# Three rotating slots for block-diagonal queries and values, and a new order of the work on every engine

## The chip, the cores and the metric

The kernel runs on one core of a Trainium2 chip. The metric is device time in microseconds (us). Three runs of the kernel before took 477.31, 477.70 and 478.84 us, the median is 477.7 us.

## What is computed

x and ctx are (16, 256, 256) in float32, so there are T = 4096 tokens of D = 256 values, in 16 heads of 16. The two steps, cut to what matters:

```
q = layernorm(x); k = v = ctx                      # heads: (b, s, 16, 16)
scores = einsum('bsqd,bskd->bsqk', q, k) / 4       # per token, between its 16 heads
scores = where(tril(16, 16), scores, -1e18)
x = x + einsum('bsqk,bskd->bsqd', softmax(scores), v)
xf = layernorm(x)
top1 = argmax(xf @ gate_w.T + gate_b)              # one of 8 experts for each token
x = x + (relu(xf @ w1[e].T + b1[e]) @ w2[e].T + b2[e])  for e = top1
```

## The kernel before

**Attention.** The tokens are cut into 16 chunks of 256 (NC, CT), four chunks make a group. A token's scores are a 16 x 16 product of its own, so eight tokens are packed into one 128 x 128 matmul: the queries of eight tokens stand as 16 x 16 blocks on the diagonal of a tile whose other places are zero, and the values likewise. Every operand is split into a float16 value and its float16 remainder ("hi" and "lo"), and three products are added. TensorE makes a chunk's scores with 96 matmuls (L1111), VectorE and ScalarE do the softmax (L684 to L702, L539), GpSimd multiplies by the inverse (L1012), TensorE turns the weights (L1129), ScalarE and VectorE split them (L544, L706), and 96 more matmuls make the chunk's outputs (L1143). VectorE adds x (L716).

**The diagonal tiles.** ScalarE and GpSimd split queries and values into qv_hl (L475, L987 for queries, L493, L1003 for values). DMAs put them onto the diagonal. Each covers 16 partitions, so eight of them serve all 128: SyncE issues five, ScalarE three (LATER). There are three diagonal slots in the arena, which later holds an expert's weights. Slots 0 and 2 hold queries of odd and even chunks, slot 1 in the middle holds the values of every chunk but the last but one. A buffer's place beside its neighbour's lets one DMA of 64 KB (spread_part, L305) carry the values of chunk i and the queries of chunk i + 2. The first two chunks' queries (L311) and the last two chunks' values (L307) go alone, 32 KB each. The joint transfer waits until outputs of chunk i - 1 and scores of chunk i are done and both operands are split:

```
sp.wait_ge(s_v_hi, i + 1)
sp.wait_ge(s_v_lo, i + 1)
if i + 2 < NC:
    sp.wait_ge(s_pv, i)
    sp.wait_ge(s_q_hi, i + 3)
    sp.wait_ge(s_q_lo, i + 3)
    sp.wait_ge(s_qk, i + 1)
```

There is one buffer of halves for values: the cast of values i waits until values i - 1 have landed in the slot (L492). There are two for queries.

**Routing.** For each group TensorE turns the outputs (L1156) and makes the gate's logits (L1171, four quarters a group). VectorE does the second layer norm and picks the expert (choose()), TensorE counts (L1178 to L1186), GpSimd scatters rows of 128 tokens to a table sorted by expert (L1050). In three stages VectorE plans which expert each of the 39 tiles (NTILES) has (plans()).

**Experts.** A tile is 128 rows of one expert. SyncE fetches rows and biases (L451 to L457), ScalarE normalizes (L566), TensorE turns the rows (L1196), ScalarE and VectorE split them (L571, L906). Eight up units of six matmuls each (L1229) make 1024 hidden values in two halves (c = 0, 1). Each half passes VectorE with the bias (hiddens(), L915), ScalarE's relu (L580) and VectorE's remainder (rests(), L926). Eight down units of two matmuls (L1245, L1246) give the result, which VectorE scales and adds in two halves (results(), L940), and GpSimd stores (L1076).

**The order.** Each engine runs its instructions in program order. Its work is written as lanes: generators that yield a number before each step, and weave() always takes the lane whose number is least. For attention the numbers are tables in the code, by lane and chunk. For the experts they are a formula, tile_at(j) = 240.0 + 5.7 j with an offset for each step: rows are turned at + 0.6, up unit n stands at + 2.6 + 0.7125 n, down unit n at + 8.65 + 0.7125 n. So ups of tile j and downs of tile j - 1 alternate one by one, and the rows of tile j are turned among the last units of tile j - 1, two up units and three down units ahead of their first use. Numbers only order the steps; what a step waits for is in its semaphores. Nothing else in a lane depends on them.

The functions that the diff touches:

## Time and profile before

| | |
|---|---|
| median of 3 runs | 477.7 us |
| span of the profiled execution, first to last instruction | 492.6 us |
| time of the profiled execution around its span | not given |
| mean granted TensorE clock | 0.962 |
| TensorE busy | 402.1 us (82%) |
| VectorE busy | 346.3 us (70%) |
| GpSimd busy | 208.7 us (42%) |
| ScalarE busy | 177.5 us (36%) |
| moved by DMA | 69.39 MB in 105162 packets |

The engines are PE (TensorE matmuls), PEld (its weight loads, which overlap the matmuls), DVE (VectorE), ACT (ScalarE), POOL (GpSimd) and SP (SyncE). "SPq" and "ACTq" mark what an engine's queue does beside operations, such as issuing a DMA. An arrow "<-" in a name has the tile written on its left and what is read on its right; in brackets behind an instruction stand the time for which its engine sat idle before it and what ended that. L305 is line 305 of the kernel. The profiled span is longer than the median run.

### The profile page before, as it was taken

What the parts mean: (1) busy time and instruction counts of PE and PEld (TensorE: products, weight loads), DVE (VectorE), ACT (ScalarE), POOL (GpSimd) and SP (SyncE); (2) the same over time, 40 slices, a digit from 0 to 9 for tenths busy, and PEclk for the clock granted to TensorE, in tenths of its full rate; (3) what the DMA queues carried; (4) which work ended last, traced back from release to release, by engine and by line L of the source; (5) the groups of instructions that cost most, each with busy time, mean ns of one, the idle gap of its engine ahead of it and who ended that gap; (6) DMA issues with size and microseconds to landing.
All of it is one profiled execution on the core that took longest, in us unless ns stands there. A gap on an engine that the chain in (4) does not pass through costs nothing.

```text
span 492.6 us, 16316 instructions
## 1 busy us (share of the span) xinstructions
PE 402.1 (82%) x5967; PEld 338.3 (69%) x5967; DVE 346.3 (70%) x777; ACT 177.5 (36%) x317; POOL 208.7 (42%) x213
## 2 busy tenths in 40 slices
PE   0135868888888866897999999779999999999992
PEld 0025757887787765896887877557778877877871
DVE  7978969789945863477757877457666666766662
ACT  3343255542624221342434433224333333433420
POOL 8345374334673467523723242642333323233221
PEclk9999999999999999975699999889999999999998
DMA  8999578899685664377612232544333322222210
GB/s 282 414 305 218 135 170 241 212 259 260 160 220 119 152 167 107 106 173 181 207 45 67 68 76 81 185 131 155 90 68 77 77 62 62 69 60 61 84 31 0
DMA packets 105162, 69.39 MB, mean 141 GB/s; under 512 B 78077, under 2 KB 88190, under 8 KB 104576
## 3 DMA queue, kind: packets, MB, share of 16 engines
q1 hardware_dynamic: 75696, 56.67, 41.9%
q10 hardware_dynamic: 25984, 3.21, 4.6%
q0 software_dynamic: 3408, 8.46, 4.6%
q8 instruction: 53, 0.87, 0.7%
q14 instruction: 21, 0.17, 0.1%
HBM read 48.28 MB, written 12.57 MB: 124 GB/s over the span
## 4 chain that ended last, share of the span: by engine, by line
PE 55%; DMA 11%; SPq 9%; DVE 9%; issue 6%; POOL 5%; ACT 2%; ACTq 1%; another core or an unknown queue 1%; POOLq 0%; DVEq 0%
PE s_ps L1229 20%; SPq L305 8%; PE at_ps L1245 6%; DMA arena<-qv_hl 6%; PE pv_ps L1245 6%; PE pv_ps L1143 6%; PE s_ps L1111 3%; PE lg_ps L1171 3%; PE pv_ps L1246 3%; PE at_ps L1246 3%; POOL qv_hl L987 2%; PE tr_ps L1156 2%; DMA arena<-x 2%; PE st_ps L1196 2%; POOL k_hl L995 1%
## 5 line engine op out<-in xcount | busy, mean ns | idle before, releaser
L1229 PEld LDWEIGHTS s_ps<-arena 128*128 x1872 | 132.7, 99 | 52.2 <-issue 14.6
L1229 PE MATMUL s_ps<-arena 128*128 128x128 f16 x1872 | 158.6, 222 | 8.4 <-DVE arena L906 5.1
L915 DVE SCALAR_TENSOR_TENSOR arena<-arena,s_ps 128x512 f32<-128x512 f32 x78 | 53.6, 687 | 48.6 <-PE s_ps L1229 35.9
L1076 POOL DMA_INDIRECT result<-arena x39 | 38.8, 995 | 95.5 <-DVE arena L940 91.6
L1111 PEld LDWEIGHTS s_ps<-k_hl,arena 128*128 128x128 f16 x1536 | 54.3, 118 | 29.9 <-DMA arena<-qv_hl 22.1
L1111 PE MATMUL s_ps<-k_hl,arena 128*128 128x16 f16 x1536 | 54.7, 179 | 23.3 <-DMA arena<-qv_hl 19.3
L1143 PE MATMUL pv_ps<-a_hl,arena 128*128 128x16 f16 x1536 | 54.7, 179 | 19.7 <-DMA arena<-qv_hl 15.9
L1143 PEld LDWEIGHTS pv_ps<-a_hl,arena 128*128 128x128 f16 x1536 | 53.5, 118 | 22.8 <-DMA arena<-qv_hl 18.3
L1245 PE MATMUL at_ps<-arena,k_in 128*128 x160 | 60.9, 383 | 0.8 <-DVE k_hl L926 0.6
L1245 PE MATMUL pv_ps<-arena,x_in 128*128 x152 | 58.1, 383 | 0.1
L1069 POOL TENSOR_TENSOR arena<-arena 128x256 f32<-128x256 f32 x39 | 30.7, 786 | 60.7 <-DMA arena<-b 60.6
L580 ACT ACTIVATE k_in<-arena 128x512 f16<-128x512 f32 x40 | 25.2, 630 | 65.7 <-DVE arena L915 60.3
L580 ACT ACTIVATE x_in<-arena 128x512 f16<-128x512 f32 x38 | 23.9, 630 | 69.0 <-DVE arena L915 60.4
L898 DVE SCALAR_TENSOR_TENSOR arena<-arena 128x512 f16<-128x512 f32 x56 | 48.0, 926 | 0.8 <-ACT arena L558 0.7
L1246 PE MATMUL at_ps<-arena,k_hl 128*128 x160 | 43.8, 274 | 0.1
L1246 PE MATMUL pv_ps<-arena,x_in 128*128 x152 | 41.8, 275 | 0.0
L1050 POOL DMA_INDIRECT sorted_rows<-pay,slot_i x32 | 34.2, 1067 | 15.9 <-DVE slot_i L802 8.1
L558 ACT ACTIVATE arena<-arena 128x512 f16<-128x512 f32 x56 | 32.0, 621 | 17.4 <-DMA arena<-w 13.7
L926 DVE SCALAR_TENSOR_TENSOR k_hl<-arena,k_in 128x512 f16<-128x512 f32 x40 | 27.7, 693 | 11.0 <-ACT k_in L580 10.7
L1003 POOL TENSOR_TENSOR qv_hl<-v_in,qv_hl 128x512 f16<-128x512 f32 x16 | 21.6, 1353 | 30.6 <-ACT qv_hl L493 30.6
L926 DVE SCALAR_TENSOR_TENSOR x_in<-arena,x_in 128x512 f16<-128x512 f32 x38 | 26.9, 709 | 8.8 <-ACT x_in L580 8.5
L987 POOL TENSOR_TENSOR qv_hl<-x_in,qv_hl 128x512 f16<-128x512 f32 x16 | 22.1, 1384 | 20.7 <-ACT qv_hl L475 20.7
(143 smaller groups left out, 614.2 us busy)
## 6 DMA issues: line engine op xcount, KB each, us to landing
arena<-w SPq DMA_DIRECT2D x28, 512.0 KB, 6.1
arena<-sorted_rows SPq DMA_DIRECT2D x39, 130.0 KB, 2.4
arena<-b SPq DMA_DIRECT2D x39, 128.0 KB
arena<-qv_hl SPq DMA_DIRECT2D x70, 64.0 KB, 3.5
k_in<-k_t SPq DMA_DIRECT2D x16, 256.0 KB, 3.9
v_in<-v_t SPq DMA_DIRECT2D x16, 256.0 KB
arena<-x SPq DMA_DIRECT2D x4, 1024.0 KB, 12.1
o_sb<-x_r SPq DMA_DIRECT2D x16, 256.0 KB, 3.8
```

What stands on the lines that cost most here:

```text
L305: eng.dma_start(to, qv_hl[part, at].rearrange("p s b c u a -> p (s b) c u a")).then_inc(s_bd[i % 2], 16)
L580: eng.activation(h_hi[j % 2][:, c * HALF:(c + 1) * HALF], h_in[:, c], ACT.Relu).then_inc(s_h_hi, 1)
L898: eng.scalar_tensor_tensor(out=lo, in0=src, scalar=W_SCALE, in1=hi, op0=ALU.mult, op1=ALU.subtract).then_inc(s_w_lo, 1)
L915: eng.scalar_tensor_tensor(out=h_in[:, c].rearrange("p (k t) -> p k t", t=P), in0=bias, scalar=W_SCALE, in1=h_ps[c][:].rearrange("p (k t) ...
L926: eng.scalar_tensor_tensor(out=h_lo[j % 2][:, cols], in0=h_in[:, c], scalar=0.0, in1=h_hi[j % 2][:, cols], op0=ALU.max, op1=ALU.subtract). ...
L1050: eng.indirect_dma_start(out=sorted_rows, out_offset=bass.IndirectOffsetOnAxis(ap=slot_i[:, b:b + 1], axis=0), in_=pay[:, b, :], in_offset ...
L1076: eng.indirect_dma_start(out=out, out_offset=bass.IndirectOffsetOnAxis(ap=rows[:, r, :].bitcast(I32)[:, D + 2:D + 3], axis=0), in_=rows[:, ...
L1111: m = eng.matmul(s[:, n], q_bd[i % 2][:, n // 2, :, n % 2, q], k_hl[:, n, k, :], start=False, stop=(n, q) == (BLK - 1, 1))
L1143: m = eng.matmul(o[:, n], v_bd[i][:, n // 2, :, n % 2, v], a_hl[:, n, a, :], start=(n, a, v) == (0, 0, 0), stop=(n, v) == (BLK - 1, 1))
L1229: k = eng.matmul(o, weights_of(j, w + k_ * H + n * P, P), xt[:, j % 2, k_ * P:(k_ + 1) * P], start=k_ == 0 and w is HI_1 and xt is xt_hi, ...
L1245: eng.matmul(y[:], h_hi[j % 2][:, n * P:(n + 1) * P], weights_of(j, at, 2 * D), start=n == 0, stop=False)
L1246: k = eng.matmul(y[:, 0:D], h_lo[j % 2][:, n * P:(n + 1) * P], weights_of(j, at, D), start=False, stop=n == KH - 1)
```

## The change

Slots: diagonal[n] are the three slots of the arena, chunk i uses diagonal[i % 3], first for its queries and, once its scores are done, for its values. Queries and values of a chunk travel in eight DMAs of 32 KB each, with separate lanes (spread_queries, spread_values). Three semaphores count landings. SyncE issues five of each eight and ScalarE three, as before.

```
-        q_bd = diagonals[:, 2 * SLOT_BLOCKS:], diagonals[:, 0:SLOT_BLOCKS]
-        v_bd = [q_bd[0] if i == NC - 2 else diagonals[:, SLOT_BLOCKS:2 * SLOT_BLOCKS] for i in range(NC)]
+        SIDES = 3
+        diagonal = [diagonals[:, n * SLOT_BLOCKS:(n + 1) * SLOT_BLOCKS] for n in (1, 2, 0)]
...
         def queries_landed(i):
-            return s_bd[i % 2], 128 * (i // 2 + 1)
+            return s_bd[i % SIDES], 128 * (2 * (i // SIDES) + 1)
 
         def values_landed(i):
-            return s_bd[i % 2], 128 * (i // 2 + 2)
+            return s_bd[i % SIDES], 128 * (2 * (i // SIDES) + 2)
...
+        def spread_part(eng, i, n, halves_of):
             part, cols = slice(HD * n, HD * (n + 1)), slice(HEADS * n, HEADS * (n + 1))
+            eng.dma_start(diagonal[i % SIDES][part, :, cols], halves_of[part]).then_inc(s_bd[i % SIDES], 16)
...
+            def spread_queries():
+                for i in range(NC):
+                    yield
+                    if i < SIDES:
+                        sp.wait_ge(*((s_zero_0, 1), (s_zero, 1), (s_zero, 2))[i])
+                    else:
+                        sp.wait_ge(s_pv, i - SIDES + 1)
                     sp.wait_ge(s_q_hi, i + 1)
                     sp.wait_ge(s_q_lo, i + 1)
+                    for n in range(8 - LATER):
+                        spread_part(eng, i, n, q_hl[i % 2])
+
+            def spread_values():
+                for i in range(NC):
+                    yield
                     sp.wait_ge(s_v_hi, i + 1)
                     sp.wait_ge(s_v_lo, i + 1)
+                    sp.wait_ge(s_qk, i + 1)
                     for n in range(8 - LATER):
-                        spread_part(eng, i, n)
+                        spread_part(eng, i, n, v_hl)
```

ScalarE's lanes change in the same way. VectorE zeroes slot 1 instead of the other slot first. Three waits differ elsewhere: the last expert's weights (load_late and weights) wait for s_pv, NC - 1 instead of s_qk, NC; fetch() waits for s_pv, NC - 2 instead of NC - 1; and hiddens() has one wait more.

```
                         dve.wait_ge(s_up, 2 * j + c + 1)
                         dve.wait_ge(s_b1[j % 2], 16 * (j // 2 + 1))
+                        dve.wait_ge(s_h_lo, 2 * (j - 1) + c + 1)
```

Order: a table TIMES holds a number for each step of each lane of each engine, for the experts too, and weave() sorts by it. The numbers serve as order alone.

```
-def weave(*lanes):
-
-    due = [(next(lane, None), n) for n, lane in enumerate(lanes)]
...
+def weave(times, **lanes):
+
+    turns = sorted((t, n, k) for n, name in enumerate(lanes) for k, t in enumerate(times[name]))
+    lane = list(lanes.values())
+    for steps in lane:
+        next(steps)
+    for _, n, _ in turns:
+        next(lane[n], None)
+    assert all(next(steps, True) for steps in lane)
```

What the sorted table gives, where the text below speaks of it:

- TensorE, attention: outputs of chunk i - 2 or i - 1 still stand about the scores of chunk i, one or two chunks deep, as before. All four quarters of the last group's gate matmuls stand ahead of the first up unit (before: one ahead, three among the first tiles' units).
- TensorE, experts: up to tile 13 ups and downs mostly alternate. From tile 14 to tile 37 a tile is: turn the rows of tile j; downs 0 to 3 of tile j - 1; ups 0 to 3 of tile j; then down 4 of tile j - 1, up 4 of tile j, down 5, up 5, down 6, up 6, down 7, up 7; and the next tile's rows. In tiles 17, 25 and 33 the run of ups is shorter.
- VectorE, experts, about the turning of tile j's rows: first half of the result of tile j - 2, second hidden half of tile j - 1, remainder of the rows (L906). In every other tile the second half of that result stands between the hidden half and the remainder, in the rest behind it. Before, the remainder stood ahead of the hidden half.

## Rows read from the trace of the kernel before

**Rows 1.** The page, chain that ended last, shares of the span by line

```profile
PE s_ps L1229 20%; SPq L305 8%; PE at_ps L1245 6%; DMA arena<-qv_hl 6%; PE pv_ps L1245 6%; PE pv_ps L1143 6%; PE s_ps L1111 3%; PE lg_ps L1171 3%; PE pv_ps L1246 3%; PE at_ps L1246 3%; POOL qv_hl L987 2%; PE tr_ps L1156 2%; DMA arena<-x 2%;
```

**Rows 2.** Busy us of each engine by stage, then clock, DMA share, GB/s

```profile
33.00:241.00 208.00, 166.44 (x3340) 152.73 (x3340) 154.83 (x366) 80.67 (x139) 104.64 (x89) 0.94 0.73 183
241.00:338.00 97.00, 89.58 (x966) 71.99 (x966) 67.17 (x167) 33.14 (x63) 39.46 (x45) 0.95 0.35 102
338.00:482.00 144.00, 142.18 (x1653) 111.72 (x1650) 95.62 (x180) 52.89 (x99) 43.93 (x49) 1.00 0.27 71
```

**Rows 3.** TensorE's waits from 35 to 240 us: us, times, longest

```profile
PE pv_ps L1143 <- DMA arena<-qv_hl: 15.9, 7, 4.4
PE s_ps L1111 <- DMA arena<-qv_hl: 8.0, 3, 3.6
```

**Rows 4.** The chain from 103 to 133 us: start, us, what

```profile
110.94 3.39 PE pv_ps L1143 x96
...
114.46 0.60 SPq L305
...
118.19 3.47 DMA arena<-qv_hl
...
121.71 3.38 PE pv_ps L1143 x96
```

**Rows 5.** Issues of spreading DMAs: median landing; on SyncE ns least/median/most

```profile
arena<-qv_hl SPq DMA_DIRECT2D x70, 64.0 KB, 3.5
...
arena<-qv_hl SPq DMA_DIRECT2D x18, 32.0 KB, 4.0
...
L305 SPq DMA_DIRECT2D arena<-qv_hl x70: 597/748/3080, 37.1 to 213.3; - x70
...
L307 SPq DMA_DIRECT2D arena<-qv_hl x10: 597/609/851, 219.9 to 230.7; - x10
```

**Rows 6.** Groups of instructions: the two steps that split the values

```profile
L493 ACT CAST qv_hl<-v_in 128x512 f16<-128x512 f32 x16 | 12.7, 791 | 18.9 <-DMA arena<-qv_hl 9.7 <-DMA v_in<-v_t 9.2
...
L1003 POOL TENSOR_TENSOR qv_hl<-v_in,qv_hl 128x512 f16<-128x512 f32 x16 | 21.6, 1353 | 30.6 <-ACT qv_hl L493 30.6
```

**Rows 7.** Timeline of TensorE where two up units stand in a row

```profile
244.51 0.97 PE L1229 MATMUL s_ps<-arena 128*128 128x128 f16 x12
245.32 1.90 PE L1171 MATMUL lg_ps<-gate_bd,o_sb 128*128 128x64 f32 x8
```

**Rows 8.** Timeline about the turning of one tile's rows in the steady part

```profile
380.50 0.50 PE L1229 MATMUL s_ps<-arena 128*128 128x128 f16 x6
380.84 0.38 PE L1245 MATMUL at_ps<-arena,k_in 128*128 x1
...
381.50 0.39 PE L1196 MATMUL st_ps<-ident,arena 128*128 128x128 f32 x2
381.72 0.38 PE L1245 MATMUL at_ps<-arena,k_in 128*128 x1
...
381.92 0.37 ACT L571 CAST arena<-st_ps 128x256 f16<-128x256 f32 x1 [0.19 <-PE st_ps L1196]
...
382.37 0.42 DVE L906 TENSOR_TENSOR arena<-st_ps,arena 128x256 f16<-128x256 f32 x1
...
383.24 0.69 DVE L915 SCALAR_TENSOR_TENSOR arena<-arena,s_ps 128x512 f32<-128x512 f32 x1 [0.45 <-PE s_ps L1229]
...
383.85 0.88 DVE L940 SCALAR_TENSOR_TENSOR arena<-at_ps,arena 128x256 f32<-128x256 f32 x2
...
387.01 0.39 PE L1196 MATMUL st_ps<-ident,arena 128*128 128x128 f32 x2
```

**Rows 9.** Timeline where TensorE waits for the remainder of a tile's rows

```profile
323.20 0.37 ACT L571 CAST arena<-st_ps 128x256 f16<-128x256 f32 x1 [3.09 <-remote]
...
323.60 0.42 DVE L906 TENSOR_TENSOR arena<-st_ps,arena 128x256 f16<-128x256 f32 x1 [2.77 <-ACT arena L571]
...
324.39 0.55 PE L1229 MATMUL s_ps<-arena 128*128 128x128 f16 x6 [2.48 <-DVE arena L906]
```

481 lines of the change are left out of this document (259 added, 222 removed), and 105 rows, old and new, of tables (TIMES, act, op1).

## Prediction

> **What bounds the kernel now.** I read the chain of work that ended last first, because it names what the end of the program hangs on. Besides TensorE it is made of the transfers that spread queries and values into the block-diagonal tiles, and of SyncE issuing them [rows 1]. Then the busy times by stage [rows 2]. From the first scores (33 us) to the first expert tile (241 us) TensorE is busy for 166.4 of 208 us, so 41.6 us are idle; from 241 to 338 us 7.4 of 97 are idle; after that 1.8 of 144. So there are two stages with different limits: attention, where TensorE waits, and the expert tiles, where almost nothing but TensorE's own stream counts.
>
> The waits of TensorE inside attention come next: 15.9 us before outputs and 8.0 us before scores, both on the spreading transfers [rows 3], together 23.9 of the 41.6 us. The chain in a stretch of attention shows why [rows 4]: outputs of one chunk end, SyncE then issues five transfers (from 114.46 to 118.8 us), the last lands 3.47 us after its issue, the next outputs run for 3.38 us and end, and so on. From one outputs to the next it is 121.71 - 110.94 = 10.77 us. The code has the reason: the values of all chunks but one share one diagonal slot, so the transfer of a chunk's values waits for the outputs of the chunk before (the wait on s_pv in spread()), and the queries of the chunk after next ride in the same transfer and wait as well.
>
> **What the change does to attention.** Three slots rotate. A chunk's queries go into slot i mod 3, and its values into the same slot once its scores are done. Outputs of chunk i-1 no longer hold up the values of chunk i, so the loop of [rows 4] is cut. This is the gain. Its bounds: at most the 23.9 us of [rows 3], at least nothing, because other loops have nearly the same length. The values still have a single buffer of halves: ScalarE's cast of chunk i waits for chunk i-1's values to have landed. That loop is cast 0.79 us, GpSimd's remainder 1.35 us [rows 6], five issues at 0.61 us and a landing of 4.0 us [rows 5], 9.2 us against 10.8. With 16 chunks the difference of 1.6 us is 25 us, the same size as the upper bound; but TensorE's own work is 166.4 / 16 = 10.4 us a chunk [rows 2], so most of the rest would have to run without a gap.
>
> The price is in the issues. Before there are 14 chunks of 8 joint transfers, 16 of first queries and 16 of last values, 144; after there are 2 x 16 x 8 = 256. A transfer of 32 KB takes SyncE 0.61 us to issue by the median, one of 64 KB 0.75 us, and the smallest are the same 0.60 us [rows 5]: halving a transfer hardly shortens its issue. SyncE goes from 70 x 0.75 + 18 x 0.61 = 63 us to 160 x 0.61 = 98 us, 35 us more; ScalarE from 56 to 96 issues, 40 x 0.61 = 24 us more, on top of 80.7 us of operations in this stage [rows 2]. Neither queue is full in 208 us, but both are in order: on ScalarE three issues (1.8 us) stand ahead of exponentials and of the halves of the weights, on SyncE five (3.1 us) ahead of loads of keys, values and x. A wait for scores ahead of each group of value transfers holds up all that is queued behind it. Cover that lies beside TensorE's work now is used up; gone altogether, the 24 us of ScalarE would be the loss. I take a gain of 7 us for attention, about a third of [rows 3]: nearer to the lower end, because the other loops and the issues follow so closely.
>
> The page on DMA of the Trainium skill (DMA: Bandwidth & Descriptors, section Rules for kernel authors) speaks against the split: it advises to coalesce small transfers, since under 64 KB one pays mostly overhead. The trace agrees in so far as a landing of 32 KB takes 4.0 us against 3.5 us for 64 KB [rows 5]; by the rule alone attention would lose instead of gaining, which is the fourth case below.
>
> **What the new order does to the expert tiles.** This part has nothing to do with slots. Until now TensorE alternates one up unit (six matmuls) with one down unit of the tile before, and turns the next tile's rows in between, two up units and three down units ahead of their use. A unit of up takes 0.34 us in that alternation (380.50 to 380.84), a tile 387.01 - 381.50 = 5.51 us [rows 8]. In the new order, from tile 14 to tile 37, a tile is: turn its rows, four downs in a row, four ups in a row, then four ups alternating with four downs. Two costs come out of it.
>
> First, ups in a row. Only the start of the expert stage shows them at full clock: two units take 245.32 - 244.51 = 0.81 us, 0.405 each [rows 7], 0.07 more than in the alternation. Three of four pay it: 0.2 us a tile.
>
> Second, the rows are turned only four downs ahead of their use. From the start of the turning, ScalarE's copy starts after 0.42 us, VectorE's remainder after 0.87 us, and it ends at 1.29 us [rows 8]; TensorE resumes about 0.37 us after the end of that operation where it has been waiting for it (323.60 + 0.42 = 324.02 against 324.39) [rows 9], so at 1.66 us. The turning (381.50 to 381.72) and four downs (0.32 us each by the rest of a pair, 381.50 - 380.84 = 0.66 less 0.34) fill 0.22 + 4 x 0.32 = 1.50 us. On VectorE a hidden half of 0.69 us stands in front, started some 0.2 us after the turning at the earliest, and half of a result (0.44 us) ahead of it; in every other tile the second half of the result (0.44 us) comes between hidden and remainder too. VectorE then reaches the remainder at about 1.0 us or 1.44 us, it ends at 1.4 or 1.86, and TensorE resumes at 1.8 or 2.2 us. Against 1.50 that is 0.3 and 0.7 us of idle TensorE, 0.5 us on average. Both costs together are 0.7 us a tile; the lower bound is nothing, if starts overlap more than these rows show. I take 0.5 us a tile, nearer to the rows, times 24 tiles: 12 us more.
>
> The other parts. Three quarters of the last group's gate matmuls move ahead of the first tile. It is the same work, up to 1.90 us a quarter [rows 7], on an engine that is busy on both sides of the boundary: no cost, but the first tile starts some 5 us later for it. The added wait on s_h_lo in hiddens() is for something that VectorE itself finished two operations before: nothing; were it not done, a tile would pay a gap of some 0.1 us. The late loads wait for the last outputs but one instead of the last scores, which costs a few us of lead before the last expert's weights; the expert inputs no longer wait for those outputs, which gives as much. At two tiles TensorE waits some 2.5 us for a remainder of rows, behind 3.09 us of ScalarE for which the trace names no engine [rows 9]; I keep these in the sum unchanged and put their 5 us into the range.
>
> **The sum.** -7 + 12 + 0 = +5 us. The profiled execution's span is 492.6 us, so 497.6; nothing of what lies around the span is shown. The median of the runs is 477.7 us, 14.9 us less than the span; I put the same +5 on it: **483 us**.
>
> **The cases.**
> 1. The forecast: attention gains about 7 us, the late order costs about 12. 483 us, by itself 478 to 488. Chance 0.40.
> 2. It ends faster: the shared slot is the one thing that held attention, TensorE's idle time there falls by 15 us of the 23.9, and the late order costs only 0.17 us a tile (4 us): 477.7 - 15 + 4 = 467 us. For it: the unbroken repetition of issue, landing, outputs in [rows 4]. Against: the 9.2 us loop of the value halves, and the rows turned late. It decides if value transfers are issued within 2 us of the scores' end and the tile's pitch stays below 5.7 us. Chance 0.33.
> 3. The wait takes another form: issues on ScalarE and SyncE eat all that the slots give, attention stays as it is, and the tiles cost 0.6 us each: 477.7 + 14 = 492 us. For it: 24 us more issues on an engine that is in the softmax chain. Against: that engine is idle for over a third of the stage. Chance 0.14.
> 4. The halved transfers land later, each by the 0.5 us between the two sizes in [rows 5]. With two landings a chunk on the path, 16 us more in place of the 7 us gained, and half the tiles' cost: 477.7 + 16 + 6 = 500 us. That is what the rule of the skill would give. Chance 0.05.
> 5. Both terms are equal, or the change does not do what it says: with the same in-order queues the rotation gives no depth and the new tile order costs nothing. 478 us. Chance 0.08.
>
> Within 0.3% (about 1.4 us) is what a measurement of this kernel cannot tell from no change. Faster by more: case 2 and a little of the others, 0.34; within: 0.09; slower: 0.57. The range runs from case 2 to case 3, 466 to 494 us; what lies outside is case 4 and the far end of case 2, with the 5 us of [rows 9] in it.
>
> **What would show it right or wrong.** In the profile after: TensorE's waits on the spreading transfers between 35 and 240 us fall from 23.9 to below 12 us, and softmax or ScalarE's casts appear in their place; the first up unit starts near 239 us: 7 us gained against the 241 us of before, 5 us of gate matmuls put ahead of it. From tile 14 on the turnings stand 5.9 to 6.1 us apart instead of 5.51, with TensorE idle for VectorE's remainder of rows in each second tile. If the pitch stays at 5.5 us, the second term is wrong and the kernel is faster; if the first up unit starts at 244 us or later, the first term is wrong.

## The result, and the profile after

The changed kernel takes **511.9 us** (median of 4 runs, 508.7 to 514.4) where the kernel before took 478.3 us beside it (4 runs, 477.3 to 481.2): a ratio of 1.068, 95% interval 1.062 to 1.073. The forecast was 483 us with a range of 466 to 494. The sign was right and the size was not: 34 us instead of 5, and 18 us beyond the end of the range. The ratios here and below compare the means of the kernels' runs in the fast state alone, so they are not the quotients of the medians beside them.

One thing had to be cleared up first. The profile shown of before has a span of 492.6 us, some 16 us more than its ordinary runs leave room for (a profiled run of the changed kernel took 508.7 us for a span of 507.0, so 1.7 us lie around it). A third profile of the kernel before (`before_third`, below) has a span of 480.6 us with a run of 482.4 us; it is the one to compare with. In the text "before" is that profile where a row of it is shown.

The page of the changed kernel, the chain that ended last, by engine and by line:

```profile
PE 57%; SPq 13%; DMA 10%; issue 5%; DVE 5%; ACT 4%; POOL 3%; ACTq 2%; POOLq 0%; DVEq 0%
PE s_ps L1379 22%; SPq L511 7%; PE at_ps L1395 7%; PE pv_ps L1395 6%; PE pv_ps L1295 5%; PE lg_ps L1321 4%; DMA arena<-qv_hl 4%; PE at_ps L1396 3%; PE s_ps L1265 3%; PE pv_ps L1396 3%; DMA arena<-w 3%; ACTq L511 2%; PE st_ps L1346 2%; PE tr_ps L1307 1%; ACT arena L731 1%
```

Against [rows 1] the landing of the spreading transfers has gone from 6% to 4%, their issue on SyncE (now L511) is 7% where it was 8%, and ScalarE's issues of them have appeared with 2%. Busy times by stage of the changed kernel (attention up to the first up, then to the turning of tile 14, then to the last downs), columns as in [rows 2]:

```profile
33.00:249.00 216.00, 171.87 (x3371) 158.27 (x3372) 155.88 (x353) 86.90 (x149) 108.47 (x91) 0.68 0.72 178
249.00:334.50 85.50, 83.25 (x927) 64.87 (x927) 63.26 (x161) 28.90 (x55) 36.82 (x41) 0.99 0.38 116
334.50:497.00 162.50, 156.68 (x1664) 117.61 (x1662) 98.51 (x179) 50.98 (x100) 49.28 (x51) 1.00 0.22 59
```

The same three stages of before, third profile:

```profile
33.00:238.50 205.50, 164.90 (x3339) 151.92 (x3337) 155.86 (x366) 81.58 (x140) 104.00 (x89) 0.83 0.74 184
238.50:323.70 85.20, 84.13 (x938) 69.02 (x939) 65.73 (x164) 32.38 (x61) 38.39 (x44) 0.97 0.38 112
323.70:471.70 148.00, 144.49 (x1688) 114.36 (x1684) 97.07 (x184) 53.71 (x101) 45.11 (x51) 1.00 0.28 73
```

In attention TensorE is idle for 216.0 - 171.9 = 44.1 us, before for 205.5 - 164.9 = 40.6. The last stage is the surprise: it is 14.5 us longer for the same work, and TensorE counts as busy for 12.2 us of it. Matmuls that follow one another slowly count as busy (the 24 of the tile shown below do, 2.02 us for what takes 4 x 0.33 = 1.3 us where ups and downs alternate), so the pitch of the tiles shows the loss and the idle time doesn't.

The yardstick for all that follows is the start of the turning of a tile's rows on TensorE, for tiles 3, 14 and 38 (by tile 3 all gate matmuls are done in both kernels, so the order of these no longer matters; what other work stands on either side of tile 3 comes below):

| profile | first up | tile 3 | tile 14 | tile 38 | mean step 3 to 14 | mean / median step 14 to 38 |
|---|---|---|---|---|---|---|
| before, third profile | 238.5 | 260.7 | 323.7 | 461.1 | 5.73 | 5.73 / 5.55 |
| changed, first profile | 249.3 | 262.7 | 334.5 | 488.1 | 6.53 | 6.40 / 6.45 |
| changed, second profile | 250.7 | 265.0 | 336.6 | 491.2 | 6.51 | 6.44 / 6.45 |

The second profile of the changed kernel (span 510.0 us, run 511.7 us) lies at its median. From before to it: 4.3 us up to tile 3, 8.5 us from tile 3 to 14, 17.2 us from tile 14 to 38, together 30.0 us; behind tile 38 it is 0.6 us quicker, which leaves the 29.4 us between the two spans. The medians lie 29.9 us apart in the job of that profile and 33.6 us in the first; 3.7 us of the first job's difference are in no profile compared here.

The first part is the least certain. Tile 3 comes between 262.7 and 269.3 us in the eight profiles of kernels that have the changed kernel's order up to it, so the 4.3 could be 2 to 9 us. And it is made of two parts: the first scores start 2.3 us later (at 35.1 us against 32.7, behind the first queries' transfer), and from there to the last outputs it is 4.3 us more (207.1 against 202.9 us). Ahead of tile 3 the changed kernel then makes 2.3 us good, in part because it has less to do there: three turnings of the last group's outputs, 0.45 us each, stand behind tile 3 instead of ahead of it.

What TensorE waits for in the changed kernel from 35 to 240 us (us in total, times, longest), the rows that answer to [rows 3]:

```profile
PE pv_ps L1295 <- DVE a_hl L870: 12.4, 6, 3.3
PE at_ps L1282 <- POOL a_sb L1166: 12.2, 5, 4.4
PE s_ps L1265 <- POOL k_hl L1151: 4.8, 2, 3.0
PE s_ps L1265 <- DMA arena<-qv_hl: 3.7, 3, 1.6
...
PE pv_ps L1295 <- DMA arena<-qv_hl: 0.7, 1, 0.7
```

The same rows of before, third profile:

```profile
PE pv_ps L1143 <- DMA arena<-qv_hl: 17.5, 9, 4.1
PE s_ps L1111 <- DMA arena<-qv_hl: 8.9, 3, 5.2
PE at_ps L1129 <- POOL a_sb L1012: 4.5, 3, 2.3
...
PE pv_ps L1143 <- DVE a_hl L706: 1.8, 1, 1.8
...
PE s_ps L1111 <- POOL k_hl L995: 0.4, 1, 0.4
```

The waits for the transfers fell from 23.9 us (26.4 in the third profile) to 4.4, as the slots should make them; the softmax, its weights and the halves of the keys took the place, 12.4 + 12.2 + 4.8 = 29.4 us where they had been 1.8 + 4.5 + 0.4 = 6.7. Who waits for the spreading transfers now is told by their own line in the changed kernel:

```profile
L511 SPq DMA_DIRECT2D arena<-qv_hl x160: 585/612/2157, 26.8 to 227.5; - x160
L511 ACTq DMA_DIRECT2D arena<-qv_hl x96: 592/632/1851, 26.3 to 223.4; - x96
...
  ACT qv_hl L680: 33.3, 12
```

L680 is ScalarE's cast of the values. It waits 33.3 us, 12 times, for the one buffer of value halves; before, it waited for the joint transfers (L305) 10.2 us, 8 times. So the wait that was cut on TensorE came back on ScalarE, ahead of the exponentials and the casts of the weights in its queue.

One tile of the changed kernel from the turning of its rows on (start, us, engine, operation):

```profile
379.27 0.39 PE L1346 MATMUL st_ps<-ident,arena 128*128 128x128 f32 x2
...
379.48 0.68 DVE L1071 SCALAR_TENSOR_TENSOR arena<-arena,s_ps 128x512 f32<-128x512 f32 x1
379.70 0.37 ACT L744 CAST arena<-st_ps 128x256 f16<-128x256 f32 x1 [1.57 <-PE st_ps L1346]
...
380.08 0.42 DVE L1096 SCALAR_TENSOR_TENSOR arena<-pv_ps,arena 128x256 f32<-128x256 f32 x1
...
380.41 0.41 DVE L1061 TENSOR_TENSOR arena<-st_ps,arena 128x256 f16<-128x256 f32 x1
...
381.19 2.02 PE L1379 MATMUL s_ps<-arena 128*128 128x128 f16 x24 [0.22 <-issue]
383.10 0.38 PE L1395 MATMUL at_ps<-arena,k_in 128*128 x1
...
385.74 0.39 PE L1346 MATMUL st_ps<-ident,arena 128*128 128x128 f32 x2
```

VectorE's remainder (L1061) stands behind a hidden half (L1071) and half of a result (L1096), ends at 380.82, and TensorE's first up starts 0.37 us later, just as read from [rows 9]. What the forecast did not have is what follows: the four ups take 383.10 - 381.19 = 1.91 us, 0.48 each, not 0.405.

### The profile page after: what moved, and what is told of

It is laid out like the page before. It is cut to its first block, busy times and chain, and to the rows that moved or that the text cites. A ratio compares the mean times of both kernels' runs of the same rounds, so it can differ in the third digit from the quotient of the medians.

```text
span 507.0 us, 16482 instructions
## 1 busy us (share of the span) xinstructions
PE 415.4 (82%) x5967; PEld 342.4 (68%) x5967; DVE 343.9 (68%) x777; ACT 175.1 (35%) x317; POOL 214.4 (42%) x213
## 3 DMA queue, kind: packets, MB, share of 16 engines
q1 hardware_dynamic: 77360, 56.74, 40.6%
## 4 chain that ended last, share of the span: by engine, by line
PE 57%; SPq 13%; DMA 10%; issue 5%; DVE 5%; ACT 4%; POOL 3%; ACTq 2%; POOLq 0%; DVEq 0%
PE s_ps L1379 22%; SPq L511 7%; PE at_ps L1395 7%; PE pv_ps L1395 6%; PE pv_ps L1295 5%; PE lg_ps L1321 4%; DMA arena<-qv_hl 4%; PE at_ps L1396 3%; PE s_ps L1265 3%; PE pv_ps L1396 3%; DMA arena<-w 3%; ACTq L511 2%; PE st_ps L1346 2%; PE tr_ps L1307 1%; ACT arena L731 1%
## 5 line engine op out<-in xcount | busy, mean ns | idle before, releaser
L1379 PEld LDWEIGHTS s_ps<-arena 128*128 x1872 | 129.1, 97 | 46.1 <-issue 18.7
L1379 PE MATMUL s_ps<-arena 128*128 128x128 f16 x1872 | 153.6, 219 | 6.2 <-issue 6.1
L1071 DVE SCALAR_TENSOR_TENSOR arena<-arena,s_ps 128x512 f32<-128x512 f32 x78 | 53.3, 684 | 50.5 <-PE s_ps L1379 50.4
L1228 POOL DMA_INDIRECT result<-arena x39 | 43.8, 1124 | 96.5 <-DVE arena L1096 95.1
L1295 PE MATMUL pv_ps<-a_hl,arena 128*128 128x16 f16 x1536 | 53.7, 179 | 14.5 <-DVE a_hl L870 12.4
L1395 PE MATMUL at_ps<-arena,k_in 128*128 x160 | 57.4, 379 | 0.9 <-DVE k_hl L1082 0.8
L1395 PE MATMUL pv_ps<-arena,x_in 128*128 x152 | 55.0, 378 | 0.8 <-issue 0.2
L1396 PE MATMUL pv_ps<-arena,x_in 128*128 x152 | 41.4, 272 | 0.0
L1082 DVE SCALAR_TENSOR_TENSOR k_hl<-arena,k_in 128x512 f16<-128x512 f32 x40 | 29.3, 734 | 14.2 <-ACT k_in L753 13.9
L1082 DVE SCALAR_TENSOR_TENSOR x_in<-arena,x_in 128x512 f16<-128x512 f32 x38 | 28.5, 750 | 14.9 <-ACT x_in L753 13.2
L1144 POOL TENSOR_TENSOR qv_hl<-x_in,qv_hl 128x512 f16<-128x512 f32 x16 | 20.8, 1300 | 28.4 <-ACT qv_hl L664 28.4
L1158 POOL TENSOR_TENSOR qv_hl<-v_in,qv_hl 128x512 f16<-128x512 f32 x16 | 21.7, 1355 | 26.2 <-ACT qv_hl L680 26.0
```

The lines of the kernel that those rows point to most:

```text
L1071: eng.scalar_tensor_tensor(out=h_in[:, c].rearrange("p (k t) -> p k t", t=P), in0=bias, scalar=W_SCALE, in1=h_ps[c][:].rearrange("p (k t) ...
L1082: eng.scalar_tensor_tensor(out=h_lo[j % 2][:, cols], in0=h_in[:, c], scalar=0.0, in1=h_hi[j % 2][:, cols], op0=ALU.max, op1=ALU.subtract). ...
L1228: eng.indirect_dma_start(out=out, out_offset=bass.IndirectOffsetOnAxis(ap=rows[:, r, :].bitcast(I32)[:, D + 2:D + 3], axis=0), in_=rows[:, ...
L1295: m = eng.matmul(o[:, n], diagonal[i % SIDES][:, n // 2, :, n % 2, v], a_hl[:, n, a, :], start=(n, a, v) == (0, 0, 0), stop=(n, v) == (BLK ...
L1379: k = eng.matmul(o, weights_of(j, w + k_ * H + n * P, P), xt[:, j % 2, k_ * P:(k_ + 1) * P], start=k_ == 0 and w is HI_1 and xt is xt_hi, ...
L1395: eng.matmul(y[:], h_hi[j % 2][:, n * P:(n + 1) * P], weights_of(j, at, 2 * D), start=n == 0, stop=False)
```

## The experiments

Times of a kernel are compared with runs of the kernel before in the same job. That kernel took 480 to 483 us (medians) in all of these jobs but the first, where it was 499.3 us (492.6 to 509.2; each job ran on a chip of its own); so for that job the ratios count. It is the job of the first three rows, its seven runs of the kernel before scattered over 17 us, and these three ratios are the least certain. The ratio of fixed_ups reaches down to 1.020.

| kernel | median us | before beside it | ratio, 95% interval |
|---|---|---|---|
| slots_alone | 526.8 | 499.3 | 1.062 (1.051 to 1.073) |
| new_tail_on_before | 524.2 | 499.3 | 1.059 (1.046 to 1.071) |
| old_tail | 513.8 | 499.3 | 1.035 (1.025 to 1.045) |
| after_again | 511.2 | 481.3 | 1.062 (1.055 to 1.069) |
| rows_earlier | 499.9 | 481.3 | 1.042 (1.036 to 1.048) |
| units_in_turn | 528.1 | 481.3 | 1.100 (1.094 to 1.107) |
| both_turns | 514.0 | 481.3 | 1.068 (1.061 to 1.075) |
| old_tail_again | 498.0 | 482.6 | 1.035 (1.026 to 1.044) |
| fixed_ups | 496.2 | 482.6 | 1.029 (1.020 to 1.037) |
| issues_on_sync | 555.4 | 482.6 | 1.154 (1.145 to 1.162) |
| halves_alone | 506.2 | 480.2 | 1.056 (1.051 to 1.061) |
| rows_earlier_all | 501.5 | 480.2 | 1.041 (1.033 to 1.048) |
| old_tail_240 | 503.1 | 480.2 | 1.048 (1.044 to 1.053) |
| earlier_and_fixed | 496.8 | 480.2 | 1.035 (1.029 to 1.040) |
| before_four | 480.7 | 481.3 | 0.999 (0.995 to 1.003) |
| after_four | 511.2 | 481.3 | 1.061 (1.054 to 1.067) |

### The kernel before and after, profiled again

No edit. The kernel before, twice:

> The kernel before, profiled a second time. Its first profiled execution has a span of 492.6 us, while its runs take 478. If that execution was an odd one (theory: the stretches from 187 to 199 and from 309 to 330 us, in which tiles took 10 us instead of 5.5, are an accident of it), this span lies at 475 to 480 us, the tiles come every 5.5 to 5.8 us from the first on, and the difference to the changed kernel's span of 507.0 is some 30 us. If they belong to the kernel, the span is again 490 or more and the runs' difference of 33 us isn't seen in the traces.

> The kernel before, profiled a third time. Its two profiles so far have spans of 492.6 and 501.6 us, while seven runs in each of two jobs took 477 to 483 us. Theory 'stalls': its two tiles of 10 us near 310 to 330 us and the one of 8 to 13 us near 250 us are in every execution; then the span is again over 490 us. Theory 'chip': where runs take 478 to 483 us the profiled span is 476 to 482 us, and tiles 11 and 12 take 6 to 7 us there.

The first of them ran on the slower chip: a span of 501.6 us, first up at 246.8, and again two steps of 12.1 and 7.9 us at tiles 11 and 12. The second: 480.6 us, and there these two steps take 5.6 and 5.9 us. So the long steps in [rows 9] belong to some executions and not to the kernel. In both of these steps, and in those of [rows 9], an engine stands for 3 to 6 us and the trace names no other engine that it waits for. From the profile on the slower chip:

```profile
313.65 4.72 another core or an unknown queue
318.39 0.38 ACT arena L571
...
321.40 5.75 another core or an unknown queue
327.18 0.70 DVE arena L915
```

GpSimd is issuing scatters of rows, one behind another, in just these stretches (seven of them start between 313.8 and 327.2 us), but what connects the two stays open. The two steps make 9.2 us of the 12.0 by which the first profile's span exceeds the third's, and 8.5 of the 21.0 for the profile on the slower chip; the rest lies elsewhere.

> The changed kernel once more, beside runs of the kernel before that took 499 us in the last job and not 478. If the chips differ by a factor, the ratio is again 1.06 to 1.07 (530 us beside 499); if what is slow on the other chip is a stretch that only the kernel before has (two tiles of 10 us at 310 to 330 us, which the changed kernel's first profile doesn't show), it is 510 to 515 us and a ratio near 1.03.

The ratio came out as the first time, 1.062 against 1.068: the size of the loss is the kernel's.

### The parts one by one: slots, attention's order, tail's order

`slots_alone` is the kernel before with the slots and the split transfers, each lane keeping its old numbers:

```diff
+                    if i < SIDES: sp.wait_ge(*((s_zero_0, 1), (s_zero, 1), (s_zero, 2))[i])
+                    else: sp.wait_ge(s_pv, i - SIDES + 1)
...
-                eng.matmul(... q_bd[i % 2] ...)
+                eng.matmul(... diagonal[i % SIDES] ...)
```

> The kernel before with three diagonal slots and a chunk's queries and values in transfers of their own, every engine's lanes in the order of before. Theory 1 (the new order of the expert lanes costs the time, the slots don't): 470 to 482 us, with TensorE's waits on DMA in the attention below 12 us instead of 23.9. Theory 2 (the slots and the halved transfers cost it: twice as many issues on ScalarE and SyncE): 495 us or more, with the loss before 240 us.

`new_tail_on_before` gives the expert lanes of the kernel before the order of the changed one:

```diff
-                        yield tile_at(j) + 2.6 + UNIT * n
+                        yield turn("PE", "ups", KH * j + n)
```

> The kernel before with the lanes of the expert tiles on ScalarE, VectorE, GpSimd and TensorE in the order of the changed kernel; two slots, the transfers and the attention's order as before (and the one wait that VectorE needs with this order). Theory 1: 503 to 515 us, tiles 6.3 to 6.5 us apart. Theory 2: 475 to 485 us. If the two parts only cost together (the tail's order needs the attention's), it is 480 to 500 us.

`old_tail` is the changed kernel with the opposite edit, the formula of before in the tables, from t0 = 232:

```diff
+    TIMES["PE"]["expert_inputs"] = at(0.6)
+    TIMES["PE"]["ups"] = at(*(2.6 + unit * n for n in range(8)))
+    TIMES["PE"]["downs"] = at(*(8.65 + unit * n for n in range(8)))
```

> The changed kernel with the lanes of the expert tiles alone (fetches, turnings, ups, downs and what VectorE, ScalarE and GpSimd do for them) back in the regular order of before, 5.7 us a tile, an up and a down in turn; the slots, the transfers and the new order of the attention stay. Theory 1 (the expert lanes' order costs nearly all: 0.87 us x 38 tiles = 33 us): 474 to 484 us, tiles 5.5 us apart. Theory 2 (the attention's part of the change costs it): 500 us or more, tiles 5.5 us apart but the first ups later than 250 us.

> The changed kernel with the expert lanes back in the regular order, once more: the first time it ran beside a kernel before of 499 us (ratio 1.035), and its profile had a single wait of 14 us for the diagonal of queries near 205 us. If that wait is the order's own (the expert lanes out of the attention leave it so), the ratio is again 1.03 or more. If it was the chip's, the ratio is 1.00 to 1.02, which leaves the tail's order as the cause of 20 us and more.

The tail's order alone costs 1.059, nearly the whole loss of 1.062 to 1.068: its steps from tile 14 to 38 are 6.44 us, as in the changed kernel, and it is slow from tile 3 on, which is taken up below. Taking the order away gives the steps back (`old_tail_again`: 5.70 mean, 5.57 median). So from tile 14 on the cause is the order of the expert lanes. Each expectation that put the other part at nothing was wrong, though: with the old tail the loss is still 1.035 in two jobs, 7.0 us up to tile 3 and 8.9 us from tile 3 to 14. (The wait of 14 us that the second expectation speaks of is at the very start, ahead of the first scores at 35 us, where before waits for 11.0 us; I had read its place wrongly. Their difference is the late start of the first scores.)

The parts don't add either: the tail's order alone costs 1.059 and the slots alone 1.062, both with the new order of attention 1.062 to 1.068. The slots in before's order cost 1.062 by themselves. The chain of `slots_alone` between 33 and 240 us was 24% SyncE's issues of spreading transfers and 6% ScalarE's; before it is 15% and not among the first dozen entries.

### The price of the issues

`halves_alone` has no new slots. Each joint transfer of 64 KB goes as two of 32 KB, at the same place and under the same waits:

```diff
-                eng.dma_start(to, qv_hl[part, at].rearrange("p s b c u a -> p (s b) c u a")).then_inc(s_bd[i % 2], 16)
+                for s in (at.start, at.start + 1):
+                    to = diagonals[part, s * SLOT_BLOCKS:(s + 1) * SLOT_BLOCKS, cols]
+                    eng.dma_start(to, qv_hl[part, s]).then_inc(s_bd[i % 2], 16)
```

> The kernel before with each diagonal transfer of 64 KB issued as two of 32 KB, the next queries and the values, one behind the other where the one was; two slots, every wait and every lane as before (112 issues more: 70 on SyncE, 42 on ScalarE). Theory 'issues': three slots in before's order cost 6 per cent for these issues alone, 20 to 30 us here too (500 to 512 us). Theory 'slots' (waits and places of the new lanes in the old order cost it, an issue is hidden): 478 to 486 us. Theory 'landing' (two transfers of 32 KB land later than one of 64 KB): attention waits on DMA grow from 26 us on TensorE, without SyncE on the chain.

506.2 us: 26 us for 112 issues, as the theory of the issues had it. The landing doesn't explain it. Issue and landing lines of `halves_alone`:

```profile
L306 SPq DMA_DIRECT2D arena<-qv_hl x140: 596/614/1723, 37.7 to 232.3; - x140
L306 ACTq DMA_DIRECT2D arena<-qv_hl x84: 592/649/1429, 37.7 to 229.3; - x84
...
arena<-qv_hl SPq DMA_DIRECT2D x158, 32.0 KB, 2.3
```

and of before, third profile:

```profile
L305 SPq DMA_DIRECT2D arena<-qv_hl x70: 597/814/4408, 37.2 to 210.3; - x70
L305 ACTq DMA_DIRECT2D arena<-qv_hl x42: 592/654/2121, 37.2 to 207.2; - x42
```

A half lands 2.3 us after its issue, where the whole took 3.5 [rows 5] (the profile has a landing for half of the issues; in slots_alone, where the halves don't go in pairs, it is 2.8 us, and for the changed kernel the page has none). But a half takes 0.61 us to issue and the whole took 0.75 to 0.81. For SyncE's five parts of a chunk that is 10 x 0.61 - 5 x 0.75 = 2.4 us more of issuing, less the 1.2 us by which the last part lands sooner: 1.2 us a chunk by these medians, some 16 us in 14 chunks. It is an estimate, and it leaves a part of the loss to what it doesn't have, such as the 42 more issues on ScalarE. TensorE's waits on these transfers grow from 26.4 to 42.5 us:

```profile
PE pv_ps L1144 <- DMA arena<-qv_hl: 29.5, 8, 7.3
PE s_ps L1112 <- DMA arena<-qv_hl: 13.0, 3, 4.5
```

and SyncE's issues rise to 31% of the chain between 33 and 240 us. The tail is that of before (median step 5.56 us against 5.55), and tile 3 comes at 281.6 us against 260.7: 20.9 of the 22.6 us between the two spans (503.2 and 480.6) are lost ahead of it. `slots_alone` has as many issues as the changed kernel and three slots, and costs the same as `halves_alone` within the intervals, so in before's order the third slot gave nothing back that the runs show.

`issues_on_sync` moves ScalarE's three issues of eight to SyncE (`LATER = 3` becomes `LATER = 0` in the changed kernel):

> The changed kernel with all eight transfers of a diagonal issued by SyncE, none by ScalarE (five and three before). Theory 'issues eat the gain': SyncE's 80 to 96 more issues at 0.65 to 0.7 us each are on the path, and the attention ends 20 to 50 us later (530 us or more). If instead ScalarE's issues are what holds back its casts and exponentials, the attention ends earlier than at 241 us and the time falls below 508 us.

555.4 us, 44 us more, for 96 issues moved: SyncE's issues become 61% of the chain between 33 and 240 us, and the first up starts at 292.3 us. ScalarE, freed of its issues, gains nothing by it, since its casts wait for the transfers:

```profile
L511 SPq DMA_DIRECT2D arena<-qv_hl x256: 585/611/2080, 28.5 to 270.6; - x128
...
  ACT qv_hl L680: 76.8, 14
```

`before_four` and `after_four` move one issue of eight the other way (`LATER = 4`):

> The kernel before with the eight transfers of a joint diagonal issued four by SyncE and four by ScalarE, where it was five and three; no more transfers than before. SyncE is on the chain of the attention for 15 per cent of it, ScalarE's queue hardly. Theory 'issues on SyncE are the path': 16 issues fewer there, 14 of them in the loop of a chunk at 0.61 to 0.8 us each, give up to 9 us, 470 to 477 us: faster than both kernels. If ScalarE's added issues hold up its casts by as much, it is 478 to 486 us.

> The changed kernel with four of the eight issues of a diagonal on ScalarE instead of three. All eight on SyncE cost 44 us more than five. Theory 'SyncE's issues are the path' on this side too: 32 issues less on SyncE give 3 to 10 us, 501 to 508 us. If ScalarE is by now as full, 511 to 518 us.

Both are the same as their parents within the interval. Taking 16 issues off SyncE was expected to give up to 9 us and gave nothing, so the price of an issue is not one of SyncE's queue alone: what SyncE is spared, ScalarE's queue pays for. Three and five was not tried, and no version that I ran beats the kernel before.

### Inside a tile: late rows, ups in a row, or the sequencer

Three edits of the changed kernel, all from tile 14 on. `rows_earlier` turns the rows two up units sooner, as before did, and leaves the runs of four:

```diff
+    for j in range(14, 39):
+        turn[j] = up[8 * (j - 1) + 6] - 0.5
+        rest[j] = hidden[2 * (j - 1) + 1] - 0.5
```

> The changed kernel, from tile 14 on with the next tile's rows turned two up units earlier on TensorE (and their remainder taken ahead of the second hidden half on VectorE); the four ups in a row stay. Theory 'late rows': this is what makes the 6.40 us of a tile out of 5.52, and they fall to 5.7 or below, 15 us off the end. Theory 'ups in a row': the four ups take 0.48 us each in a row and 0.33 us of time in turn with a down, so the tile keeps its 6.1 to 6.4 us and the end moves by 6 us at most.

`units_in_turn` interleaves the four downs and the four ups behind the turning, and leaves the turning late:

```diff
+        turns = sorted(up[a:a + 4] + down[b:b + 4])
+        down[b:b + 4], up[a:a + 4] = turns[0::2], turns[1::2]
```

> The changed kernel, from tile 14 on with the four downs and the four ups behind each turning taken in turn (down, up, down, up) and not four and four; the rows are turned where the change has them. Theory 'ups in a row': 0.6 us a tile come back, 25 x 0.6 = 15 us. Theory 'late rows': the first up now stands behind one down instead of four, waits for the rows 1 us longer, and the tile takes 6.4 us or more, up to 7.2.

`both_turns` has both:

> Both of these edits together, which is the regular order of before on TensorE from tile 14 on. Either theory: tiles of 5.5 to 5.7 us from tile 14 on, 17 to 21 us off the end. If the tiles keep 6.2 us or more, it is neither, and the order of VectorE's or ScalarE's lanes holds them.

`fixed_ups` takes the register arithmetic out of the ups (every tile's first layer uses expert 0's place):

```diff
-                                k = eng.matmul(o, weights_of(j, w + k_ * H + n * P, P), xt[...
+                                at = w + k_ * H + n * P
+                                k = eng.matmul(o, arena[:, at:at + P], xt[...
```

> The changed kernel, in which every tile's first layer takes its weights from the place of expert 0 at fixed addresses (so the result's first layer is that of another expert); everything else, the order too, stays. An up unit is then 12 instructions on TensorE's sequencer instead of 16. Theory 'ups in a row are bound by the sequencer': the four ups fall from 1.9 to 1.3 us, the tile from 6.40 to 5.8 us, 15 us off the end. Theory 'late rows' alone: the first up still waits for the rows, the four behind it run at 0.33 us each for want of register work, and what is gained is this alone, 0.3 to 0.6 us a tile. If ups are bound by the matmuls themselves, the time stays at 511 us.

> The changed kernel with the rows turned earlier from tile 14 on and the first layer's weights of expert 0 at fixed addresses (another expert's first layer is computed). Each edit alone took 0.53 us off a tile of 6.44 us. Theory 'one fault' (the rows arrive late, TensorE's sequencer stands at the first up and its register work for four ups in a row comes after it): together they give little more than each alone, 5.6 to 5.9 us a tile, 493 to 497 us. Theory 'two faults': they add up, 5.4 us a tile, 484 to 488 us.

| steps from tile 14 to 38, us | mean | median |
|---|---|---|
| before, third profile | 5.73 | 5.55 |
| changed (after_again) | 6.44 | 6.45 |
| rows_earlier | 5.92 | 5.75 |
| fixed_ups | 5.91 | 5.87 |
| earlier_and_fixed | 5.89 | 5.59 |
| both_turns | 6.43 | 6.33 |
| units_in_turn | 7.00 | 7.00 |

By the medians, which leave out single long steps: late rows are worth 6.45 - 5.75 = 0.70 us a tile, and the run of four 5.75 - 5.55 = 0.20 us. "Late rows" is the main cause, and "ups in a row" as a cause of its own is only the 0.20. That is 0.90 us a tile, though the 24 tiles lost 17.2 us, 0.72 a tile: before has single long steps there (its mean is 0.18 us above its median) and the changed kernel hardly has. By the means, late rows are 6.44 - 5.92 = 0.52 us and the run 5.92 - 5.73 = 0.19. How much ScalarE has to wait for the turned rows says it in one line each, before, changed (first profile) and rows_earlier:

```profile
  ACT arena L571: 9.1, 35
```

```profile
  ACT arena L744: 51.1, 37
```

```profile
  ACT arena L756: 27.6, 37
```

(engine and line that waited for the turning, us, times). In `rows_earlier` the four ups stand in a row as in the changed kernel, but take 350.23 - 348.65 = 1.58 us, 0.395 each, not 1.91:

```profile
348.65 1.69 PE L1391 MATMUL s_ps<-arena 128*128 128x128 f16 x24
350.23 0.38 PE L1407 MATMUL pv_ps<-arena,x_in 128*128 x1
```

That is the 0.405 of [rows 7]. The difference, 0.33 us, comes from waiting ahead of the run. In the compiled program an up unit is 16 instructions on TensorE (four of register arithmetic for the weights' addresses, six weight loads, six matmuls), a down unit 5. In the trace of the tile above the sequencer stands at the semaphore for the rows from 380.11 to 380.87 us and works out no address in that time, and afterwards an address comes every 0.11 us between the matmuls: 16 instructions in 0.48 us are what it gives. `fixed_ups` bears this out: without the register work the ups run at 0.33 us each even behind a wait of 0.79 us,

```profile
403.48 0.84 PE L1380 MATMUL s_ps<-arena 128*128 128x128 f16 x12 [0.79 <-issue]
404.15 0.38 PE L1396 MATMUL at_ps<-arena,k_in 128*128 x1
```

(two units, 404.15 - 403.48 = 0.67 us). And the two edits don't add: by the means 0.52 and 0.53 us each and 0.55 together, by the medians 0.70 and 0.58 each and 0.86 together. It is mostly one fault, not two: the late rows make the wait, and the register work makes it dearer.

`units_in_turn` is slower than the changed kernel because one down (0.33 us) is now all that covers the turning, and the wait comes into the open. From tile 14 on TensorE waits 28.0 us for the remainder, in 25 tiles; the total, and one of them:

```profile
PE s_ps L1391 <- DVE arena L1073: 28.0, 25, 1.8
...
400.31 0.55 PE L1391 MATMUL s_ps<-arena 128*128 128x128 f16 x6 [1.29 <-DVE arena L1073]
```

So the four downs in a row were the cover for the late rows, not a fault of their own. `both_turns` was expected at 5.5 to 5.7 us and takes 6.33: in the trace the first up comes 406.48 - 404.35 = 2.13 us after the turning, behind two ups and two downs, with a wait of 0.43 us in front of it that is put down to no engine. `rows_earlier` has a lead of 354.66 - 351.88 = 2.78 us. The kernel before gets by with 372.94 - 371.07 = 1.87 us and no wait, so the order of VectorE's and ScalarE's lanes around the turning has a share in it too; that was not tried apart.

`rows_earlier_all` does the same from tile 4 on:

> The changed kernel with the rows turned two up units earlier from tile 4 on, not only from tile 14 on. From tile 14 on this gave 0.52 us a tile. Theory: the tiles 4 to 13 have the same fault, 6.5 us for 5.7 with the same cause, so 10 x 0.5 = 5 us more come back: 493 to 496 us. If they are held by the last group's routing and the fill rows instead, it is 499 us as with rows_earlier.

It is the same as `rows_earlier` within the intervals, and tiles 3 to 14 take 6.34 us a step instead of 6.51: 2 us of the 5 expected. Its profile comes to tile 3 at 269.3 us, 5.9 us after that of `rows_earlier`, which hides these 2 us in the time.

`old_tail_240` starts the regular order later:

> The changed kernel with the expert lanes in the regular order starting at 240 us, as before, where old_tail started them at 232 us. old_tail took 16 us more than the kernel before: 7 us up to its fourth tile and 9 us in its tiles 3 to 14, where the last group's planning stands between the tiles' steps. If these 9 us come of the shift of the tiles against the planning, it is 487 to 491 us; if of the attention part of the change, 498 us. The kernel before is beaten only if both go.

503.1 us, no better than from 232 (498.0 us, in another job), and the steps from tile 3 to 14 stay at 6.6 us. So the place of the tiles against the planning isn't it.

What the 8.5 us between tiles 3 and 14 are, the traces say when the stretch is cut at tile 8 (us):

| profile | tile 3 to 8 | tile 8 to 14 |
|---|---|---|
| before, third profile | 27.6 | 35.5 |
| before_again (other chip) | 27.6 | 44.8 |
| halves_alone | 27.6 | 35.8 |
| changed (after_again) | 33.1 | 38.5 |
| new_tail_on_before (other chip) | 33.6 | 46.2 |
| old_tail_again | 30.0 | 42.0 |
| rows_earlier_all | 29.9 | 39.8 |

Of the 5.6 us up to tile 8, 1.4 us are the three turnings of outputs that stood ahead of tile 3 before, and 1.3 us are four downs that the later turning of the rows puts ahead of the mark. The rest is late rows again, with less cover than from tile 14 on. In tile 3 two downs, and in tiles 4 and 5 a single one, stand with a turning of outputs between the rows' turning and the first up, and TensorE waits 0.5 to 0.6 us each time. Tile 4:

```profile
271.88 0.39 PE L1346 MATMUL st_ps<-ident,arena 128*128 128x128 f32 x2
272.11 0.61 PE L1307 MATMUL tr_ps<-ident,o_sb 128*128 128x128 f32 x4
272.56 0.38 PE L1395 MATMUL at_ps<-arena,k_in 128*128 x1
...
273.49 0.56 PE L1379 MATMUL s_ps<-arena 128*128 128x128 f16 x6 [0.45 <-issue]
```

`rows_earlier_all` gets 3.2 us of the 5.6 back (1.0 of them because its earlier turnings leave two ups and a down behind the mark), and `new_tail_on_before`, which has before's attention, loses 6.0 us here against before_again on the same chip. So up to tile 8 the cause is the order of the expert lanes too. From tile 8 to 14 the changed kernel loses 3.0 us, 2.0 of them in the ups (19.3 us for 48 against 17.3): runs of ups begin before tile 14, six in a row in tile 8 and eight in tile 11, at 0.46 to 0.48 us each. `rows_earlier_all` doesn't give the 3.0 us back, and `old_tail_again` loses 6.5 us there, in other steps (tiles 11 to 13 take 6.9, 9.5 and 6.9 us). In the changed kernel's second profile the fetches of rows (SyncE's issues and sorted_rows) stand on the chain of that stretch, and before's doesn't show them there. What they cost was not tried.

## Why the prediction was wrong

**Reading of what bounds the kernel: right.** TensorE waited for the spreading transfers, and with three slots these waits fell from 23.9 to 4.4 us; below 12 us, with softmax in their place, is what came.

**Attention, -7 us: wrong, measured +4.3 us** (tile 3 at 265.0 against 260.7; the last outputs end 6.6 us later). The step that failed is "cover that lies beside TensorE's work now is used up", which set the price of 112 more issues below the gain. They cost 26 us when nothing else changes (halves_alone), 0.23 us each, because SyncE's queue was part of the loop of a chunk already [rows 1, 4]: ten issues of 0.61 us instead of five of 0.75 are 2.4 us more on a loop of 10.8, and the sooner landing gives only 1.2 of them back. I had counted 35 us more on SyncE against 208 us and called the queue not full; a queue need not be full to be on the path. The loop through the single buffer of value halves was named, at 9.2 us, and it is the wait that came (from 10.2 to 33.3 us on ScalarE). The new order of attention hides most of the 26 us: where the slots in the old order bring tile 3 21.7 us later (289.3 us against 267.6, on one chip), 4.3 to 7.0 us are left. What that order would give without the split was not tried, so how much the third slot itself is worth stays open.

**The landing, case 4: wrong in its mechanism.** The halves landed sooner in the kernels whose profiles show it, 2.3 and 2.8 us against 3.5, so [rows 5], where the few 32 KB transfers took 4.0 us, misled: those were the first two chunks' queries and the last two chunks' values. The rule of the Trainium skill (DMA: Bandwidth & Descriptors, Rules for kernel authors), to coalesce below 64 KB, pointed the right way all the same: splitting was dear, 26 us for 112 issues more, by its issues.

**The expert tiles from tile 14, +12 us: right in mechanism, too small, measured +17.2 us** (24 x 0.72). Ups in a row at 0.2 us a tile is what the runs give. The working had 0.5 us for the late rows, all of it idle TensorE, and measured were 0.52 (0.70 by the medians), of which only 0.31 is idle time behind the four downs, 0.4 and 0.1 in turn instead of 0.7 and 0.3. What the working missed is the run behind the wait: 0.48 us an up instead of 0.395 to 0.405, 0.33 us a tile, as the sequencer can't prepare it ahead. So the 0.7 us that both costs came to in the working is near the 0.72 measured by luck: an idle time too long stood in for slow ups, and before's long steps took off another 0.18. The step that failed in the forecast is the next one, 0.5 us for both "if starts overlap more than these rows show": no row showed such an overlap. The first up starts 0.37 us after the remainder, as worked out, and the forecast steps of 5.9 to 6.1 us were 6.4.

**Tiles 3 to 13: left out, measured +8.5 us.** The term was counted "from tile 14 to tile 37" because only there the pattern is regular, so the price list ended where the pattern ended. The same fault stands in tiles 3 to 8. The output turnings there were part of the last group's work, which the prediction moved the other way, ahead of the first tile. And ups and downs don't alternate up to tile 13, as the section on the change has it: tiles 8 and 11 have runs of six and eight ups, and the ups are 2.0 of the 3.0 us lost from tile 8 on.

**The gates, the added wait, the late loads: costed at nothing.** None was tried apart. The first ups to tile 3 take 14.3 us instead of 22.2, as the gates' move says, and the 5 us of [rows 9] belong to the executions.

**What would prove it wrong** was stated as a first up at 244 us or later: it came at 249.3. The rival that was nearest is case 3, issues that eat all that the slots give, 492 us with a chance of 0.14; its mechanism, attention losing what the slots give to the issues, is the one that came, and attention lost 4.3 us where the case had none.

The sum by what was measured: 4.3 + 8.5 + 17.2 = 30.0 us, of 33.6 us between the medians of the first job and 29.9 between those of the second profile's job.

## What to carry to other kernels

When a change splits a transfer, price the issues on the queue that is in the loop, one by one, before counting what the landing gains: here 112 issues took 26 us though no queue was full. When an order is rewritten, ask for each value how long before its use it is made, and keep that lead; the four downs behind the late turning covered most of it and still left 0.5 to 0.7 us a tile. Read the loss of a stage that is always busy by the pitch of its tiles, since a TensorE that waits for its sequencer between matmuls counts as busy. And look at where a loss lies before two equal sums are given one cause: 8.5 us in the changed kernel and 8.9 us in old_tail_again, both between tiles 3 and 14, stand in different tiles.

## What was not expected of the hardware

Ups in a row run at 0.395 us when the sequencer is ahead, at 0.48 us behind a wait, and at 0.33 us without register arithmetic or in turn with downs; the same six matmuls each time. A transfer of 32 KB in pairs landed after 2.3 us, where 64 KB in one took 3.5. The same kernel took 478 to 483 us in five jobs and 499 us in one, on another chip; whether the chip is the reason one job can't tell. And the granted clock, which was 0.68 in the attention of the changed kernel's first profile (the lower of the two levels, 1.2 GHz, for over half of it) and 1.00 in its second, made no difference there: outputs of the last chunk ended at 240.7 and 242.2 us.
